# A transformer block on one core: the feed-forward's y turned by DMA, its tail spread over three engines, and two stage borders rewoven

## The chip, the cores and the metric

The program runs on one core of one Trainium2 chip. The metric is device microseconds for one execution. Before the change three runs gave 1199.7, 1199.9 and 1201.7 us, median 1199.9.

The engines are called PE (TensorE, matrix products and transposes), DVE (VectorE), ACT (ScalarE), POOL (GpSimd) and SP (SyncE, which here only issues transfers). Each works through its own list of instructions in order and waits on semaphores that the others raise.

## The reference, cut to what matters

64 images of 224 x 224 x 3 go through a patch embedding, one attention layer with fake quantisation and one feed-forward layer with activations rounded to 8 bits and ternary weights. There are 197 tokens of 192 values per image.

```python
h = _L0_tok_ref(x, W, b)                      # 196 patches an image -> 192 values
h = concatenate([cls_tok, h])                 # 197 tokens
h = h + _L0_attn_ref(_layernorm(h), ...)      # 12 heads of 64, every tensor fake-quantised
h = h + _L0_ffn_ref(_layernorm(h), ...)

def rmsnorm(x, g):          return x * rsqrt(mean(x*x) + 1e-6) * g
def activation_quant(x):    scale = 127 / max(max|x|, 1e-5);  return clip(round(x*scale), -128, 127) / scale
def weight_quant(w):        scale = 1 / max(mean|w|, 1e-5);   return clip(round(w*scale), -1, 1) / scale
def bitlinear(x, w, g):     return activation_quant(rmsnorm(x, g)) @ weight_quant(w).T
def _L0_ffn_ref(x, w_in, g_in, w_out, g_out):
    up, gate = split(bitlinear(x, w_in, g_in))     # 192 -> 2 * 512
    return bitlinear(silu(gate) * up, w_out, g_out)   # 512 -> 192
```

## The kernel before, in words

The three layers are three stages, each handed over through memory.

**Embedding, to about 215 us.** Fifteen packs of token tiles (SEQ; the last two are JOIN and LAST). For each tile PE sums six float32 products, DVE adds the bias and takes statistics, and DVE and POOL turn it into the quantised x. Each pack stores x (`x_int`) and h plus a bias (`h_res`), one transfer a tile. ACT issues the stores of the packs up to JOIN - 1, SP those of JOIN and LAST (`store_pack` of SP, lines 457 to 463: six transfers of x, then six of h).

**Join, about 215 to 255 us.** The first images of the attention stage are woven in beside the last packs. The attention's buffers lie over the embedding's (`big`), so after image step 1 DVE waits until every store of h and x has landed (lines 1113 to 1115) before it goes on with step 2.

**Attention, to about 860 us.** A software pipeline over images, `image_step(b)`: projections of image b + 1 or b + 2, scores and exponentials of b, softmax sums, normalising of b - 2 (line 1061), weighted values of b - 3, output projection of b - 4 and b - 5, and POOL adds the result into `h_res` in memory with an accumulating transfer (line 762). SP loads the turned x with a transposing transfer (`load_xT`, line 466), stores the inverse sums and loads them spread over all partitions (lines 485 and 492).

**Passage, about 860 to 920 us.** The last image steps (B to B + 4, with B = 64) only drain. The first steps of the feed-forward are placed between them by hand, engine by engine (the calls `images(...)` and `pairs(...)` at the end of each engine's block). SP loads the first `tin` only after all its image steps (lines 529 to 531).

**Feed-forward, to the end.** 50 pairs of 128-token tiles (the last holds 64 tokens). `pair_step(t)` is a software pipeline again: in one step, pair t gets its statistics and is centred, t - 1 its factors and zi, t - 2 is turned on PE and copied out, t - 3 goes through the 192 to 1024 product, silu, y, its square and y times g_out (yg), t - 4 gets the factors of y and yi (y rounded to int16), t - 5 is turned on PE (line 1297), copied out, multiplied by the output weights and given its residual (line 1043), t - 6 is stored. A step's work on DVE ends the factors with four tiny instructions (lines 968 to 979); ft (line 979) holds the factors that take the results of the products back to real size.

One ACT instruction (line 645) copies the turned x and the turned y together out of PSUM. Eight products that nobody reads (line 1322) follow each step on PE.

## Time and profile before

| | |
|---|---|
| median of three runs | 1199.9 us |
| the profiled execution, its own time | 1200.62 us |
| its span, first to last instruction | 1198.6 us |
| busy: PE, DVE, ACT, POOL | 1107.8, 1055.8, 923.2, 452.7 us |
| mean granted clock of TensorE | 0.977 |
| read from and written to HBM | 143.11 and 36.12 MB |

The shares over the whole span say little, because the stages differ: ACT does nothing in the first 190 us, and PE is busy almost throughout since fill-in products are among its work. Read the stages apart. A start in the timeline is in us from the first instruction. Engines overlap the end of one instruction with the start of the next by some 0.1 us, so what an instruction costs its engine is the distance between two starts and not quite its duration.

### The profile page before, as it was taken

The numbers are of one execution on the slowest core, as the hardware profiler recorded it, in microseconds if no ns is written. First come the engines' busy times: TensorE is split into PE (matmuls) and PEld (weight loads), VectorE is DVE, ScalarE is ACT, GpSimd is POOL, SyncE is SP. The second block draws the span as 40 slices with busy tenths as digits, with TensorE's granted clock in tenths as the row PEclk, the third lists the DMA queues.
The fourth block names the chain that finished last, engine by engine and source line by source line (L and its number), as shares of the span: only waits on it lengthen the run. The fifth ranks groups of instructions, "written<-read, shape, count | busy, mean of one in ns | idle before, by whom it ended". The sixth has DMA issues, their size and how long they took to land.

```text
span 1198.6 us, 31970 instructions
## 1 busy us (share of the span) xinstructions
PE 1107.8 (92%) x11182; PEld 674.8 (56%) x11182; DVE 1055.8 (88%) x2028; ACT 923.2 (77%) x1831; POOL 452.7 (38%) x486
## 2 busy tenths in 40 slices
PE   7999999879999999999999999999857888888888
PEld 6999998435555555555555555555433444444444
DVE  7687566479999999999999999999988999999996
ACT  0000002869999999999999999999738999999997
POOL 5644343102221123322111122121237777776774
PEclk9999999979999999999999999999958999999999
DMA  8998998336555566566655555555542333333332
GB/s 291 315 311 252 315 304 230 113 117 149 151 150 150 150 149 149 147 151 150 153 149 148 146 153 149 147 154 144 141 99 65 101 101 106 102 103 100 98 94 71
DMA packets 158436, 187.87 MB, mean 157 GB/s; under 512 B 42864, under 2 KB 119808, under 8 KB 158080
## 3 DMA queue, kind: packets, MB, share of 16 engines
q1 hardware_dynamic: 117408, 158.10, 42.4%
q0 software_dynamic: 15360, 9.70, 8.7%
q10 hardware_dynamic: 25536, 18.31, 4.7%
q8 instruction: 83, 1.36, 0.5%
q14 instruction: 49, 0.40, 0.1%
HBM read 143.11 MB, written 36.12 MB: 150 GB/s over the span
## 4 chain that ended last, share of the span: by engine, by line
PE 73%; ACT 10%; issue 8%; DVE 3%; DMA 2%; SPq 2%; POOL 2%; ACTq 0%; DVEq 0%; POOLq 0%
PE psum L1128 14%; PE psum L1186 12%; PE psum L1249 12%; PE psum L1219 7%; PE psum L1189 7%; PE psum L1202 6%; PE psum L1236 6%; PE psum L1307 5%; ACT yi L673 3%; ACT zi L681 2%; ACT big L666 2%; PE psum L1297 1%; DMA big<-xt 1%; PE psum L1287 1%; POOL big L790 1%
## 5 line engine op out<-in xcount | busy, mean ns | idle before, releaser
L1061 DVE TENSOR_TENSOR pi<-big 128x2364 int16<-128x2364 f32 (+1 forms) x128 | 333.5, 2605 | 10.1 <-DMA big<-z_row 9.8
L762 POOL DMA_DIRECT2D h_res<-att x128 | 142.0, 1214 | 526.4 <-ACT att L600 517.3
L624 ACT ACTIVATE big<-psum 128x788 f32<-128x788 f32 (+1 forms) x384 | 330.4, 862 | 3.0 <-PE psum L1236 2.6
L586 ACT ACTIVATE qki<-psum 128x394 int16<-128x394 f32 x384 | 172.5, 509 | 26.6 <-PE psum L1189 14.8
L1128 PE MATMUL psum<-big 128*128 128x192 f32 (+1 forms) x1128 | 185.1, 327 | 2.2 <-DMA big<-xt 2.0
L1128 PEld LDWEIGHTS psum<-big 128*128 128x128 f32 (+1 forms) x1128 | 180.3, 188 | 5.5 <-DMA big<-xt 2.6
L1249 PE MATMUL psum<-big,sa_hot 128*32 128x197 f32 (+1 forms) x3072 | 170.1, 339 | 7.9 <-DVE zt L1085 7.9
L586 ACT ACT_TABLE_LOAD x1 | 1.3, 1283 | 189.8 <-PE psum L1189 189.8
L790 POOL TENSOR_TENSOR big<-big,goutb 128x512 f32<-128x512 f32 (+1 forms) x99 | 123.7, 1270 | 55.5 <-DVE big L1033 55.5
L1236 PE MATMUL psum<-qkb 64*128 64x197 bf16 (+1 forms) x1536 | 129.7, 247 | 0.0
L595 ACT ACTIVATE vi<-psum 128x384 int16<-128x384 f32 (+1 forms) x256 | 115.7, 529 | 12.9 <-PE psum L1189 12.7
L1219 PE MATMUL psum<-big,vb 128*64 128x197 bf16 (+1 forms) x1536 | 105.7, 261 | 17.4 <-issue 15.5
L605 ACT ACTIVATE oi<-psum 128x394 int16<-128x394 f32 x192 | 102.8, 535 | 22.4 <-PE psum L1219 22.4
L851 DVE TENSOR_SCALAR big<-pi,lo,hi 128x2364 bf16<-128x2364 int16 (+1 forms) x128 | 115.0, 898 | 2.5
L1186 PE MATMUL psum<-xT,w1b 128*128 128x394 bf16 x384 | 105.8, 335 | 5.5 <-ACT qki L586 2.1
L1249 PEld LDWEIGHTS psum<-big,sa_hot 128*32 128x32 f32 (+1 forms) x3072 | 81.4, 110 | 50.9 <-issue 8.8
L1307 PE MATMUL psum<-winb,big 96*128 96x512 bf16 (+1 forms) x396 | 98.8, 394 | 0.0
L1219 PEld LDWEIGHTS psum<-big,vb 128*64 128x64 bf16 (+1 forms) x1536 | 63.0, 112 | 58.5 <-issue 55.6
L1322 PE MATMUL psum<-winb,big 96*128 96x512 bf16 x400 | 94.6, 379 | 0.0
L1236 PEld LDWEIGHTS psum<-qkb 64*128 64x128 bf16 (+1 forms) x1536 | 76.7, 104 | 30.8 <-issue 12.0
L860 DVE TENSOR_TENSOR big<-psum,tokb 128x192 f32<-128x192 f32 x98 | 34.4, 351 | 56.4 <-PE psum L1128 55.9
L1186 PE MATMUL psum<-w1b,xT 128*128 128x384 bf16 (+1 forms) x256 | 73.2, 338 | 8.2 <-ACT vi L595 1.4
(107 smaller groups left out, 1800.6 us busy)
## 6 DMA issues: line engine op xcount, KB each, us to landing
big<-z_row SPq DMA_DIRECT2D x192, 394.0 KB, 5.1
big<-xt SPq DMA_DIRECT2D x98, 384.0 KB, 4.5
tin<-h_res SPq DMA_DIRECT2D x49, 192.0 KB, 2.9
tres<-h_res SPq DMA_DIRECT2D x49, 192.0 KB, 2.5
out<-oo SPq DMA_DIRECT2D x49, 192.0 KB, 2.6
h_res<-big ACTq DMA_DIRECT2D x84, 96.0 KB, 4.4
h_res<-att POOLq DMA_DIRECT2D x64, 96.0 KB, 3.3
x_int<-big ACTq DMA_DIRECT2D x84, 64.0 KB, 4.2
```

Source lines behind the costliest of these rows:

```text
L586: act.activation(qki[:, k, :, :], psum[:, bank, 0:2 * N] .rearrange("p (c n) -> p c n", c=2), ACT.Copy, scale=factor[(F_Q, F_K)[b % 2]])\
L595: act.activation(vi[0:r, ip, t, half * W:(half + 1) * W], psum[0:r, bank, 0:W], ACT.Copy, scale=factor[F_V]).then_inc(evac[kind], 1)
L624: act.activation(ex[0:r, tri, t, 4 * g:4 * g + 4, :].rearrange("p (a h) n -> p a h n", a=2), psum[0:r, 2 * t:2 * t + 2, 0:2 * N] .rearrang ...
L762: pool.dma_start(h_res[bass.ds(b - 4, 1), t0:t0 + r, :].rearrange("a n d -> (a n) d"), att[0:r, par, t, :], accum_op=ALU.add).then_inc(s_a ...
L790: g.tensor_tensor(yg[0:r, oth, a, :], yy[0:r, a, 0:HID], goutb[0:r, :], ALU.mult)\
L1061: v.tensor_tensor(pi[0:r, t, :, 0:N], ex[0:r, it, t, :, :], zb[0:r, ip, :, :], ALU.mult).then_inc(s_pi, 1)
L1128: last = mm(psum[p0:p0 + r, bank_of_tile(i, s), 0:D], xring[:, s, c * 128 + p0:c * 128 + p0 + r], weight_of(cls, c), start=(c == 0), stop= ...
L1186: mm(psum[rows, bank, 0:n], left[:, 0], right[:, 0], start=True, stop=False)
L1219: last = mm(psum[i * DH:(i + 1) * DH, bank, c * N:(c + 1) * N], vb[0:r, (tri + d) % 3, t, head * DH:(head + 1) * DH], pT[0:r, im % 2, t, j ...
L1236: last = mm(psum[0:r, 2 * (w % 2) + i % 2, (i // 2) * N:(i // 2 + 1) * N], qk[po:po + DH, 6 + c, t0:t0 + r], qk[po:po + DH, c, 0:N], start ...
L1249: last = mm(psum[32 * j:32 * j + 32, 4, 0:N], sa_hot[0:r, w // 2, :], ex[0:r, it, t, 4 * (w // 2) + j, :], start=(w == 0), stop=(w == 5))
L1307: last = mm(psum[0:r, 2 * a + half, :], zT3[:, oth, a, c, 0:r], winb[:, c, half * HID:(half + 1) * HID], start=(c == 0), stop=(c == 1))
```

## The change

Five things are changed together.

1. y is turned by a transposing transfer of SP (from yi3 in SBUF to yTi, int16, laid over `qki`) in place of eight PE transposes. DVE converts it to bfloat16 (yT3, a single buffer) two steps later. ACT's copy takes the turned x alone. The pipeline is a step deeper (LAGS 8).
2. The output of a pair goes to two PSUM banks. DVE scales and adds tile 0 as before. ACT scales tile 1 into `osc` at the end of its step, and POOL adds the residual to it a step later.
3. POOL makes `ft` in place of DVE.
4. At the join, POOL issues the h stores of JOIN and LAST. DVE's wait for all stores moves from ahead of image step 2 to just ahead of the first write of the probabilities in it.
5. At the passage, the feed-forward's steps 0 to 5 are placed elsewhere among the last image steps, the first `tin` is loaded after image step B - 1, ACT loads the silu table ahead of its pair steps, and PE gets fill-in products in image steps B + 1 and B + 2 and in pair steps 0 to 2.

```diff
@@ SP
-                sp.wait_ge(s_hp, i + 1)
-                for s in range(PACK):
-                    sp.dma_start(tile_rows(h_res, i, s), hp[:, i % 2, s, :]).then_inc(s_h1[i % 2], 16)
...
+                if pair(5) or pair(7):
+                    wait_apart(sp, s_t["o_ready"], ...t - 6)
+                    wait_apart(sp, s_t["o_added"], ...t - 6)
+                if at := pair(5):
+                    sp.dma_start(tres[0:r, oth, 0:n, :], pair_rows(h_att, t - 5, r, n)).then_inc(s_t3b[oth], 16)
+                if at := pair(7):
+                    sp.dma_start(pair_rows(out, t - 7, r, n), oo[0:r, oth, 0:n, :]).then_inc(s_t3o[oth], 16)
+                if at := pair(4):
+                    wait_apart(sp, s_t["yi"], t - 3)
+                    wait_apart(sp, s_t["yT_read"], t - 5)
+                    sp.dma_start_transpose(yTi[:, par, 0:4 * n, 0:r], yi3[0:r, par, 0:n, :].rearrange("p a h -> p (a h)"))\
+                      .then_inc(s_ym[par], 16)
-            images(image_step, 0, B + 4)
+            images(image_step, 0, B - 1)
             wait_added(sp, 0)
             sp.dma_start(tin[:, 0, :, :], pair_rows(h_att, 0, 128, 2)).then_inc(s_t3[0], 16)
+            images(image_step, B, B + 4)
@@ ACT
-                    act.activation(zyT[:, par, :], turned.bitcast(i16)[:, 512:2048], ACT.Copy)\
+                    act.activation(zT3[:, par, 0:n, :, 0:r], psum[0:KH, 4, :].bitcast(i16)[:, 0:512]..., ACT.Copy)\
                        .then_inc(s_t["xT_read"], 1)
+                if (at := pair(6)) and at[1] == 2:
+                    act.wait_ge(s_t["o_summed"], t - 5)
+                    act.activation(osc[:, par, :], psum[:, 5, 0:D], ACT.Copy, scale=ft[:, (q + 2) % 4, 1, 1:2])\
+                       .then_inc(s_t["o_scaled"], 1)
+            act.activation(table[0:1, :], fac[0:1, 0:1], ACT.Silu)
@@ POOL
+                if i >= JOIN:
+                    pool.wait_ge(s_hp, i + 1)
+                    for s in range(PACK):
+                        pool.dma_start(tile_rows(h_res, i, s), hp[:, i % 2, s, :]).then_inc(s_hlast, 16)
+                if (at := pair(7)) and at[1] == 2:
+                    g.tensor_tensor(oo[:, oth, 1, :], osc[:, oth, :], tres[:, oth, 1, :], ALU.add)\
+                        .then_inc(s_t["o_added"], 1)
+                if pair(1) or pair(4):
+                    wait_apart(pool, s_t["step"], 3 * t - 1)
+                    g.tensor_tensor(ft[:, q, :, :], pt[:, oth, A127, :, :], wdeq4[:, :, :], ALU.mult)\
+                        .then_inc(s_t["dequant"], 1)
@@ DVE
-                        v.tensor_tensor(ft[:, q, :, :], V(A127), wdeq4[:, :, :], ALU.mult).then_inc(s_t["dequant"], 1)
+                if at := pair(6):
+                    dve.wait_ge(s_ym[par], loads_of(t - 6, par))
+                    wait(dve, s_t["o_summed"], t - 6)
+                    v.tensor_copy(yT3[:, 0:n, :, 0:r].rearrange("p a c n -> p (a c) n"), yTi[:, par, 0:4 * n, 0:r])\
+                     .then_inc(s_t["yT_read"], 1)
-                    for a in range(n):
-                        ins = v.scalar_tensor_tensor(oo[0:r, oth, a, :], psum[0:r, 6, a * D:(a + 1) * D], ...)
+                    v.scalar_tensor_tensor(oo[0:r, par, 0, :], psum[0:r, 6, 0:D], ft[0:r, (q + 2) % 4, 1, 0:1],
+                                           tres[0:r, par, 0, :], ALU.mult, ALU.add).then_inc(s_t["o_ready"], 1)
+                    if image == 0 and t == 0:
+                        dve.wait_ge(s_hlast, 32 * PACK)
+                        for p in range(2):
+                            dve.wait_ge(s_h1[p], stores_at(JOIN - 1 - (JOIN - 1 - p) % 2))
+                            dve.wait_ge(s_x1[p], stores_at(LAST - (LAST - p) % 2))
@@ PE
+                    if b in (B + 1, B + 2):
+                        pe.wait_ge(s_exp, U1 * B)
+                        keep_busy(3, 12)
-                        for c in range(4):
-                            last = nc.tensor.transpose(dst[:, a, c, 0:r], yi3[...], ident[0:r, 0:r])
-                    last.then_inc(s_t["yT_summed"], 1)
```

SP's list at the join, before (`xT` is the turned x of an image, `z_row` the inverse softmax sums, `x_int` and `h_res` the stores of a pack):

```order
L460 DMA x_int<-big 32x4x256 x6
L463 DMA h_res<-big 32x4x192 x6
L466 DMA_TRANSPOSE xT<-x_int 128x2x208
L485 DMA z_row<-zinv 4x197 x3
L492 DMA big<-z_row 128x788 x3
L460 DMA x_int<-big 32x4x256 x6
L463 DMA h_res<-big 32x4x192 x6
L466 DMA_TRANSPOSE xT<-x_int 128x2x208
```

And the same place now:

```order
L463 DMA x_int<-big 32x4x256 x6
L466 DMA_TRANSPOSE xT<-x_int 128x2x208
L486 DMA z_row<-zinv 4x197 x3
L493 DMA big<-z_row 128x788 x3
L463 DMA x_int<-big 32x4x256 x6
L466 DMA_TRANSPOSE xT<-x_int 128x2x208
```

Twelve issues have left SP's list; they stand in POOL's, six behind each of its last two packs.

DVE's list over one steady step of the feed-forward, before, from the residual of one step to the last factor of the next:

```order
L1043 SCALAR_TENSOR_TENSOR oo<-psum,ft,tres 128x192 x2
L998 BN_STATS st<-tin 128x6 x2
L1003 TENSOR_REDUCE pt<-zc 128x2
L1009 BN_AGGR mv<-st 128x2 x2
L1015 TENSOR_REDUCE pt<-big 128x1 x2
L968 TENSOR_TENSOR pt<-pt 128x4
L988 SCALAR_TENSOR_TENSOR zc<-tin,mv,ginb 128x192
L971 TENSOR_SCALAR pt<-pt 128x4
L988 SCALAR_TENSOR_TENSOR zc<-tin,mv,ginb 128x192
L974 RECIPROCAL pt<-pt 128x4
L979 TENSOR_TENSOR ft<-pt,wdeq 128x4
L977 TENSOR_TENSOR pt<-pt 128x4
```

And the same stretch now:

```order
L1069 SCALAR_TENSOR_TENSOR oo<-psum,ft,tres 128x192
L1020 CAST big<-qki 128x1024
L1026 BN_STATS st<-tin 128x6 x2
L1031 TENSOR_REDUCE pt<-zc 128x2
L1037 BN_AGGR mv<-st 128x2 x2
L1043 TENSOR_REDUCE pt<-big 128x1 x2
L991 TENSOR_TENSOR pt<-pt 128x4
L1010 SCALAR_TENSOR_TENSOR zc<-tin,mv,ginb 128x192
L995 TENSOR_SCALAR pt<-pt 128x4
L1010 SCALAR_TENSOR_TENSOR zc<-tin,mv,ginb 128x192
L998 RECIPROCAL pt<-pt 128x4
L1001 TENSOR_TENSOR pt<-pt 128x4
```

The conversion stands right behind the residual of the step before and ahead of the statistics, one of two residual instructions is gone, and so is line 979.

POOL's list over one steady step now (it was the same without lines 799 and 803):

```order
L783 TENSOR_TENSOR pt<-pt,neg_half 128x2
L789 TENSOR_SCALAR pt<-mv 128x2
L792 TENSOR_TENSOR pt<-pt,neg_half 128x2
L799 TENSOR_TENSOR oo<-big,tres 128x192
L803 TENSOR_TENSOR ft<-pt,wdeq 128x4
L811 TENSOR_TENSOR big<-big,goutb 128x512 x2
```

The residual of tile 1 and the factors stand between the powers and the two products with g_out.

## Rows read from the trace of the kernel before

**Rows 1.** Windows: start:end, us, busy us (instructions) of each engine, PEclk, DMA share, GB/s.
```profile
245.80:254.00 8.20, 7.85 (x60) 2.91 (x60) 8.13 (x8) 4.02 (x8) 0.00 (x0) 0.50 0.36 133
...
1020.00:1050.00 30.00, 26.55 (x185) 14.08 (x184) 28.30 (x92) 29.54 (x57) 20.93 (x25) 1.00 0.35 100
```
**Rows 2.** Waits, 205 to 262 us: who, for whom, us in all, times, longest.
```profile
DVE vb L851 <- DMA h_res<-big: 13.0, 1, 13.0
ACT vi L595 <- PE psum L1189: 12.7, 4, 8.6
```
**Rows 3.** Timeline of SP's queue at the join: start, us, instruction.
```profile
233.10 1.30 SPq L492 DMA_DIRECT2D big<-z_row  x3
234.45 4.00 SPq L460 DMA_DIRECT2D x_int<-big  x6
238.49 4.69 SPq L463 DMA_DIRECT2D h_res<-big  x6
```
**Rows 4.** Page, part 6: engine, op, count, KB each, median us from issue to landing.
```profile
big<-z_row SPq DMA_DIRECT2D x192, 394.0 KB, 5.1
```
**Rows 5.** Timeline of POOL's accumulating stores, two at a time.
```profile
856.95 2.63 POOL L762 DMA_DIRECT2D h_res<-att  x2 [6.30 <-ACT att L600]
864.14 1.78 POOL L762 DMA_DIRECT2D h_res<-att  x2 [4.57 <-ACT att L600]
```
**Rows 6.** Timeline of DVE at the passage.
```profile
880.57 0.62 DVE L998 BATCH_NORM_STATS2 st<-tin 128x6 f32<-128x192 f32 x2 [3.51 <-DMA tin<-h_res]
...
899.45 0.75 DVE L1033 SCALAR_TENSOR_TENSOR big<-psum,ft,big 128x512 f32<-128x512 f32 x1
...
920.46 1.41 DVE L1033 SCALAR_TENSOR_TENSOR big<-psum,ft,big 128x512 f32<-128x512 f32 x2
```
**Rows 7.** Timeline of ACT over one steady step.
```profile
1041.20 1.43 ACT L645 ACTIVATE big<-psum 128x1536 bf16<-128x1536 int16 x1
...
1043.67 1.34 ACT L673 ACTIVATE yi<-big,pt 128x512 int16<-128x512 f32 x2
...
1047.02 1.43 ACT L645 ACTIVATE big<-psum 128x1536 bf16<-128x1536 int16 x1
```
**Rows 8.** Timeline of POOL and DVE in the same step.
```profile
1047.39 0.69 POOL L773 TENSOR_TENSOR pt<-pt,neg_half 128x2 f32<-128x2 f32 x1 [0.54 <-ACT ysq L693]
...
1049.33 0.16 DVE L977 TENSOR_TENSOR pt<-pt 128x4 f32<-128x4 f32 x1
```
**Rows 9.** Waits, 960 to 1136 us (30 steps).
```profile
POOL big L790 <- DVE big L1033: 32.3, 30, 1.3
...
DVE pt L968 <- POOL pt L773: 7.9, 30, 0.4
```
**Rows 10.** Groups by line: shapes, count, busy us, mean ns of one, idle before.
```profile
L1043 DVE SCALAR_TENSOR_TENSOR oo<-psum,ft,tres 128x192 f32<-128x192 f32 x60 | 22.0, 408 | 0.0
...
L728 POOL TENSOR_TENSOR big<-big 128x192 f32<-128x192 f32 (+1 forms) x24 | 14.3, 594 | 13.4 <-DMA big<-w_tok 11.6
```
**Rows 11.** Single lines: duration ns min/median/max, first and last start, forms.
```profile
L651 ACT ACTIVATE big<-psum x4: 255/593/593, 894.8 to 1181.4; 96x512 bf16<-96x512 int16 x3, 96x128 bf16<-96x128 int16 x1
L907 DVE TENSOR_SCALAR woutb<-big x1: 359/359/359, 182.1 to 182.1; 128x768 bf16<-128x768 int16 x1
L907 DVE TENSOR_SCALAR winb<-big x1: 690/690/690, 132.8 to 132.8; 96x2048 bf16<-96x2048 int16 x1
```
**Rows 12.** DVE beside POOL at the join (timeline).
```profile
220.62 2.62 POOL L748 TENSOR_TENSOR big<-big,bb2b 128x1152 f32<-128x1152 f32 x1
222.22 1.66 DVE L851 TENSOR_SCALAR qkb<-qki,lo,hi 128x2364 bf16<-128x2364 int16 x1 [1.47 <-ACT qki L586]
...
230.76 0.90 DVE L851 TENSOR_SCALAR qkb<-qki,lo,hi 128x2364 bf16<-128x2364 int16 x1 [2.03 <-ACT qki L586]
```
**Rows 13.** The transposing load of x (line 466, 64 times), issue to landing.
```profile
DMA to landing us min/median/max: 2.5/5.6/7.1
```
**Rows 14.** Timeline of ACT at the end.
```profile
1194.23 0.39 ACT L657 ACTIVATE big<-psum 128x256 bf16<-128x256 int16 x1 [1.79 <-PE psum L1297]
```

More of the change, by code:

```diff
@@ L367, in pair_of, with over_pairs @@
             return pair
-        def over_pairs(eng, step):
+        def over_pairs(eng, step, start=None):
             first = 14
-            for t in range(EARLY, first):
+            for t in range(start or EARLY, first):
                 step(t, t % 2, t % 4)
@@ L1310, in pair_step @@
                         last.then_inc(s_t["hid"], 1)
-                if at := pair(5):
+                if at := pair(6):
                     r, n = at
-                    y_turned(t)
-                    wait(pe, s_t["o_ready"], t - 5)
+                    pe.wait_ge(s_t["yT_read"], t - 5)
+                    wait(pe, s_t["o_ready"], t - 6)
+                    wait(pe, s_t["o_scaled"], t - 6)
                     for a in range(n):
                         for c in range(4):
-                            last = mm(psum[0:r, 6, a * D:(a + 1) * D], yT3[:, par, a, c, 0:r], woutb[:, c, :],
+                            last = mm(psum[0:r, 6 - a, 0:D], yT3[:, a, c, 0:r], woutb[:, c, :],
                                       start=(c == 0), stop=(c == 3))
                     last.then_inc(s_t["o_summed"], 1)
-                if (pair(5) or pair(3)) and (not isinstance(t, int) or t > EARLY):
-                    for _ in range(8):
-                        mm(psum[:, 7, :], zT3[:, oth, 0, 0, :], winb[:, 0, 0:HID], start=True, stop=True)
+                if not isinstance(t, int) or EARLY <= t <= NPAIR + 2:
+                    keep_busy(7, 8)
+                elif t < 3:
+                    keep_busy(3, 4)
             for i in (JOIN, LAST):
```

154 lines of the change are left out of this document (69 added, 85 removed).

## The prediction

> **What bounds the kernel now.** I read the windows first, then the waits of the places where they show a gap, then single steps in the timeline. Three places matter.
>
> At the join nothing but transfers holds the chip: DVE stands 13.0 us until the last store of h has landed, and ACT 8.6 us behind it [rows 2]. The stores of the last pack leave SP one by one, six of x in 4.00 us and then six of h in 4.69 us [rows 3]. PE stands too, and the granted clock in the 8.2 us behind that gap is 0.50 (1.2 of 2.4 GHz), with ACT busy for only 4.02 us of them [rows 1].
>
> At the passage DVE stands 3.51 us for the first `tin`, with the last image's normalising queued behind it. Then the feed-forward needs 21.0 us, from 899.45 to 920.46, for its first three steps [rows 6].
>
> In the steady feed-forward ACT is busy 29.54 of 30 us [rows 1]. A step is the distance between two copies of line 645, 1047.02 - 1041.20 = 5.82 us [rows 7]. But there are two more limits just as close, and they decide what relief of ACT is worth:
> - A circle through three engines. yi starts when the factors are done. From yi to the end of the squares is 3.35 us (1043.67 to 1047.02) plus 0.1 for the last accumulator [rows 7]. The power on POOL starts at 1047.39, 0.28 us later, and from its start to the start of the last factor instruction are 1.94 us, with 0.16 for that one [rows 8]. Sum 3.45 + 0.28 + 1.94 + 0.16 = 5.83 us, which is the whole step.
> - DVE: it waits 7.9 / 30 = 0.26 us a step for that power [rows 9], so its own list takes 5.82 - 0.26 = 5.56 us.
>
> POOL waits 32.3 / 30 = 1.08 us a step for y [rows 9].
>
> **The join.** Twelve issues leave SP. Of these the six of pack LAST stood ahead of the landing that DVE waited for, and the six of JOIN ahead of everything else. On POOL the six of LAST cost up to 6 x 1.3 = 7.9 us (half of 2.63 each) from the end of the h add at 223.2 [rows 5, 12], so they are issued by 231 and landed by 236. The last stores are then those of x. The spread load of the inverse sums, at 233.10, waited for its own chain (the inverse sums, stored and landed) and hardly moves. Six x stores behind it end at 238.4, as now, and land by 241 [rows 3]. DVE no longer stands ahead of step 2: it does the conversion of v and turns the softmax sums at about 234, which is what PE stood for. Its first normalising waits for the spread load, 233.1 + 1.3 + some 4 = 238.5 (5.1 us from issue [rows 4]), in place of 246.3. I expect ACT's 8.6 us back and half of the 4 us that it lost at the low clock, against 1 to 3 us that it will wait for the next spread load: 8.5 us, bounds 5 and 11.
>
> POOL's stores write descriptors beside DVE's conversions; two accumulating stores took 2.63 us once against 1.78 [rows 5]. The Trainium skill speaks against this edit: by "SBUF — State Buffer", section "SBUF: two separate sides", GpSimd can't write descriptors while DVE is in a two-port mode. By it the six would end some 4 us later, at 235, still ahead of the x stores, so the sum is the same.
>
> **The passage.** `tin` is loaded early, which takes out the 3.51 us [rows 6]. Pairs 0, 1 and 2 move ahead of the last normalisings or between them: 1.5 + 2.3 + 2.3 us of DVE work that stood behind them, so the last probabilities come only some 1.5 us later than now, while the first 192 to 1024 product is ready to run as soon as the last values are done. The table load of 1.3 us leaves the path. By this the first y ends 4 to 6.5 us earlier (the range is the clock of that product, 1.7 or 3.5 us). The three steps that took 21.0 us would take 17.5 at the steady pace; I count 1 us of these 3.5 as won. Together 6 us, bounds 2 and 9. The fill-in products cost nothing where PE has nothing to do; if they stood ahead of work that is ready they would cost 12 x 0.21 us.
>
> **ACT in the steady step.** The copy of 1536 columns, 1.43 us, becomes one of 512 columns, 0.59 [rows 7, 11]. The scaling of tile 1 is new: 192 columns, by the distance per column between these two rows 0.3 to 0.45; I take 0.38. ACT's list is then 5.82 - 0.84 + 0.38 = 5.36 us. That alone frees 0.46 us.
>
> **DVE in the steady step.** One residual instruction goes, 22.0 / 60 = 0.37 us [rows 10], and ft, 0.1. The conversion of 1024 columns is new. The nearest rows are 0.36 us for 768 columns and 0.69 for 2048 [rows 11]; I take 0.42. DVE's list is 5.56 - 0.47 + 0.42 = 5.51 us.
>
> It can also be held. Beside POOL's add of 1152 columns (220.62 to 223.24) a conversion of 2364 columns took 1.66 us, alone 0.90 [rows 12]: it did its work only when POOL was nearly through, some 0.2 us ahead of POOL's end. The new conversion comes 1.0 us after the first y, and just then POOL is 0.9 us into the first of two products with g_out, 1.27 us each. I count 0.1 to 0.4 us of hold, as much as the rest of the first product, so 5.6 to 5.9 us.
>
> The same rule is in the Trainium skill, "SBUF — State Buffer", section "Who interferes with whom": the pair of ports is locked for a whole instruction, and the one that comes second is blocked. Our row agrees but for the 0.2 us at the end. It also says this for a DVE instruction with two SBUF inputs beside a reading one of GpSimd, which would touch the centring and POOL's new add; by it the step would be longer by up to the add's 0.5 us where they meet.
>
> **POOL in the steady step.** The add of 192 columns costs 0.59 [rows 10], the factors 0.2, both inside the 1.08 us that it waits for y [rows 9]. Some 0.2 us is left, and with the three register writes of the waits perhaps none. When the first product with g_out starts later, the conversion is held longer.
>
> **The circle.** Of its terms only ft leaves, 0.1: 5.73 us. So the step can't fall below about 5.7 whatever ACT gains. With DVE at 5.6 to 5.9, and POOL full, I take a step of 5.83 us, no change: 43 steps x 0 = 0, bounds 43 x -0.12 = -5 and 43 x +0.3 = +13.
>
> **The transfers.** A transposing load of x lands 5.6 us after issue, 2.5 at least [rows 13]. The new one has 2.5 times the elements. It has from yi in one step to the conversion two steps on, over 8 us, and SP has three other issues of 0.4 us a step. Bound below 0; above, if it takes SP over 4 us to issue, `tin` comes late and the step grows by as much. I take 0.
>
> **The end.** One more step, and the last turn goes through a transfer: 5 us in place of 2.2 (1.79 for PE and 0.39 for the copy [rows 14]). +2.5 us, bounds 1 and 5.
>
> **Sum.** 1200.6 (the profiled execution) - 8.5 - 6 + 0 + 2.5 = 1188.6. That execution is 0.7 above the median, so 1188.
>
> **Rivals.**
> - A, the step falls to the circle's 5.7: the conversion meets no product, or is held for 0.1. Then 1188 - 5 = 1183. For it: the hold is short by the rows. If the circle too gives way since the engines shift against each other, and ACT's list decides at 5.4, it is 43 x -0.4 = -17: 1171. Against it: the three engines' sums are all within 0.3 us.
> - B, slower: the conversion is held through both products with g_out. These stand back to back, and if POOL takes the second before DVE gets in, the hold is 1.4 us and DVE's list 6.9 to 7.1. The step becomes 7.1: 43 x 1.3 = +56, 1244. For it: the rows show only a single POOL instruction, never two, and the conversion waits at this place in every step. Against it: DVE has asked first, and POOL seems to let go 0.2 us ahead of its end. From a hold of 0.28 us a step above my forecast (12 / 43) on the change loses.
> - C, in between: POOL's new add meets the centring and the last factor in each step, or SP's transfer makes `tin` late. +0.35 us a step, +15: 1203.
> - D, the join gives little, since the next spread load (its chain begins behind the x stores) stops DVE again: -3 in place of -8.5, 1194.
>
> **Chances.** Forecast with D 0.57, A 0.22 (of it 0.05 for 1171), C 0.11, B 0.10. 0.2% is 2.4 us, about what can be told from no change here. Faster 0.81, same 0.05, slower 0.14. The range from 1173 to 1206 leaves out B, the lowest part of A and a little of C.
>
> **What would show it.** Right: the gap of ACT at 240 us is under 3 us; the first y of pair 0 comes 13 to 16 us earlier; steps of line 1060 are 5.7 to 5.95 us apart; the conversion's mean is 0.5 to 0.8 us, above the 0.42 that it needs, and POOL's wait for y is near 0. Wrong: a mean of the conversion over 1.5 us (B); DVE waiting for `tin` or for the turned y (the transfers); ACT with no idle time at a step of 5.4 (A's lower part); any gap over 5 us at the join.

## The result, and the profile after

| | before | after |
|---|---|---|
| median on the same chip | 1200.8 us | 1215.7 us |
| the profiled execution, its own time | 1200.62 us | 1215.72 us |
| its span | 1198.6 us | 1213.9 us |
| mean granted clock | 0.977 | 0.962 |

The ratio of the times is 1.0127, with an interval from 1.0108 to 1.0145. The forecast was 1188 us, 12 us faster than before, with a range from 1173 to 1206. The change is 15 us slower: wrong in sign.

The two spans differ by 15.3 us. Three instructions of DVE exist in both traces and split this sum: the last normalising of the attention (885.66 before, 880.73 after), and the first and the last y (899.45 and 1188.01 before, 890.65 and 1198.26 after).

| part | before to after | forecast |
|---|---|---|
| join: the last normalising starts earlier | -4.9 | -8.5 (5 to 11) |
| passage: the first y against it, 13.8 to 9.9 us | -3.9 | -6 (2 to 9), 1 of it in the first three steps behind |
| 49 steps of the feed-forward, 288.6 to 307.6 us | +19.0 | 0 (-5 to +13) |
| from the last y to the end, 10.6 to 15.6 us | +5.0 | +2.5 (1 to 5) |

**The join.** DVE's timeline and SP's queue after the change (start, us, instruction, idle time before it):

```profile
239.34 2.62 DVE L1090 TENSOR_TENSOR pi<-big 128x2364 int16<-128x2364 f32 x1 [1.28 <-DMA big<-z_row]
...
248.31 0.41 DVE L1120 STREAM_TRANSPOSE zinv<-zti 128x224 f32<-128x224 f32 x1
252.51 2.62 DVE L1090 TENSOR_TENSOR pi<-big 128x2364 int16<-128x2364 f32 x1 [3.79 <-DMA big<-z_row]
```
```profile
233.72 3.86 SPq L463 DMA_DIRECT2D x_int<-big  x6
241.89 1.24 SPq L466 DMA_TRANSPOSE xT<-x_int  x1
243.22 1.67 SPq L486 DMA_DIRECT2D z_row<-zinv  x3
245.98 1.29 SPq L493 DMA_DIRECT2D big<-z_row  x3
```

The 13.0 us of DVE [rows 2] are gone and the first normalising starts 7.0 us earlier. The second starts only 4.2 us earlier. DVE had its inverse sums ready at 238.06 (the trace has L1120 at 237.65 for 0.41), but SP issued nothing until 241.89, since its wait for all stores stands there, then issued the load of xT, and only then stored the sums.

**The steady step.** The windows, in the form of [rows 1]:

```profile
1000.00:1060.00 60.00, 48.94 (x263) 25.00 (x262) 58.00 (x162) 50.83 (x115) 48.34 (x67) 0.89 0.55 135
```

ACT has 9 us of idle time in 60, as the change meant it to have. DVE is busy 58.0 of 60. The granted clock is 0.89, where it was 1.00 before [rows 1]; e8 below asks whether that matters. One step on DVE, from y to y:

```profile
1038.29 1.41 DVE L1060 SCALAR_TENSOR_TENSOR big<-psum,ft,big 128x512 f32<-128x512 f32 x2
1039.62 0.41 DVE L1069 SCALAR_TENSOR_TENSOR oo<-psum,ft,tres 128x192 f32<-128x192 f32 x1
1039.94 0.81 DVE L1020 CAST big<-qki 128x1024 bf16<-128x1024 int16 x1
1040.67 0.61 DVE L1026 BATCH_NORM_STATS2 st<-tin 128x6 f32<-128x192 f32 x2
...
1041.81 1.24 DVE L1043 TENSOR_REDUCE pt<-big 128x1 f32<-128x512 f32 x2
1043.18 0.16 DVE L991 TENSOR_TENSOR pt<-pt 128x4 f32<-128x4 f32 x1
...
1043.69 0.41 DVE L1010 SCALAR_TENSOR_TENSOR zc<-tin,mv,ginb 128x192 f32<-128x192 f32 x1
1044.02 0.17 DVE L998 RECIPROCAL pt<-pt 128x4 f32<-128x4 f32 x1
1044.23 0.35 DVE L1001 TENSOR_TENSOR pt<-pt 128x4 f32<-128x4 f32 x1
1044.50 0.75 DVE L1060 SCALAR_TENSOR_TENSOR big<-psum,ft,big 128x512 f32<-128x512 f32 x1
```

That is 6.21 us without a wait. POOL and ACT in the same step:

```profile
1039.20 2.67 POOL L811 TENSOR_TENSOR big<-big,goutb 128x512 f32<-128x512 f32 x2 [0.71 <-DVE big L1060]
1042.21 0.70 POOL L783 TENSOR_TENSOR pt<-pt,neg_half 128x2 f32<-128x2 f32 x1 [0.33 <-ACT ysq L691]
...
1043.27 0.69 POOL L792 TENSOR_TENSOR pt<-pt,neg_half 128x2 f32<-128x2 f32 x1
1043.93 0.62 POOL L799 TENSOR_TENSOR oo<-big,tres 128x192 f32<-128x192 f32 x1
```
```profile
1038.48 1.33 ACT L671 ACTIVATE yi<-big,pt 128x512 int16<-128x512 f32 x2 [0.86 <-DVE pt L1001]
...
1044.61 0.72 ACT L671 ACTIVATE yi<-big,pt 128x512 int16<-128x512 f32 x1 [0.73 <-DVE pt L1001]
```

Two meetings can be read here. The conversion (1039.94) comes while POOL is in its first product (1039.20 to 1040.5) and lasts 0.73 us to the next start. And the last factor instruction, four columns wide, comes while POOL's add runs (1043.93 to 1044.55) and ends with it at 1044.58. yi waits for just that instruction. Two instructions of this kind can also run side by side: the centring (L1010, two inputs in SBUF) started at 1043.69, 0.42 us into POOL's power (1043.27, 0.69 us), and took its usual 0.41. The groups of 28 steps (960 to 1136 us):

```profile
L1020 DVE CAST big<-qki 128x1024 bf16<-128x1024 int16 x28 | 20.9, 748 | 0.0
...
L799 POOL TENSOR_TENSOR oo<-big,tres 128x192 f32<-128x192 f32 x28 | 16.9, 604 | 0.0
...
L1001 DVE TENSOR_TENSOR pt<-pt 128x4 f32<-128x4 f32 x28 | 11.3, 403 | 1.0
```

403 ns for L1001, where the same instruction (L977) took 0.16 before [rows 8]. In all 30 steps from 950 to 1140 us it ended 0.01 to 0.03 us behind POOL's add.

**The end** shows the hold of the conversion most plainly, since there it once meets a product and once nothing. DVE, then POOL:

```profile
1199.25 1.37 DVE L1020 CAST big<-qki 128x1024 bf16<-128x1024 int16 x1
...
1202.81 0.42 DVE L1020 CAST big<-qki 128x1024 bf16<-128x1024 int16 x1
...
1209.12 0.41 DVE L1069 SCALAR_TENSOR_TENSOR oo<-psum,ft,tres 64x192 f32<-64x192 f32 x1 [3.60 <-DMA out<-oo]
```
```profile
1199.08 1.26 POOL L811 TENSOR_TENSOR big<-big,goutb 64x512 f32<-64x512 f32 x1 [0.96 <-DVE big L1060]
1200.35 0.69 POOL L783 TENSOR_TENSOR pt<-pt,neg_half 64x1 f32<-64x1 f32 x1
```

The same conversion takes 0.42 us alone and 1.37 when it starts 0.17 us behind POOL's product. It ended at 1200.62, 0.28 us behind the product. If its 0.42 us of work stand at its end, it began them 0.14 us ahead of the product's end. The last residual also waits 3.60 us for an earlier store.

**The passage.** In three steps from the first y (890.65, 897.00, 903.37, 912.65) the last has 9.3 us. POOL:

```profile
906.82 3.65 POOL L772 DMA_DIRECT2D h_res<-att  x4
909.15 2.08 POOL L783 TENSOR_TENSOR pt<-pt,neg_half 128x2 f32<-128x2 f32 x1
```

Four accumulating stores stand in a row ahead of a power, and DVE waited 3.38 us for it (its L991 started at 911.42).

### The profile page after: what moved, and what is told of

Its sections match the earlier page's. It is cut to its first block, busy times and chain, and to the rows that moved or that the text cites. A ratio compares the mean times of both kernels' runs of the same rounds, so it can differ in the third digit from the quotient of the medians.

```text
span 1213.9 us, 31866 instructions
## 1 busy us (share of the span) xinstructions
PE 1105.7 (91%) x10814; PEld 668.1 (55%) x10814; DVE 1081.0 (89%) x1976; ACT 900.2 (74%) x1877; POOL 502.0 (41%) x600
## 4 chain that ended last, share of the span: by engine, by line
PE 67%; DVE 14%; issue 8%; DMA 4%; ACT 3%; POOL 3%; SPq 1%; DVEq 1%; ACTq 0%; POOLq 0%
PE psum L1154 14%; PE psum L1212 12%; PE psum L1275 12%; PE psum L1245 7%; PE psum L1215 7%; PE psum L1228 6%; PE psum L1262 6%; DVE pt L1043 3%; DVE big L1060 2%; DVE big L1020 2%; PE psum L1324 2%; POOL big L811 1%; DVE zc L1010 1%; DVE st L1026 1%; DMA big<-xt 1%
## 5 line engine op out<-in xcount | busy, mean ns | idle before, releaser
L772 POOL DMA_DIRECT2D h_res<-att x128 | 138.8, 1196 | 501.8 <-ACT att L609 492.6
L811 POOL TENSOR_TENSOR big<-big,goutb 128x512 f32<-128x512 f32 (+1 forms) x99 | 132.3, 1357 | 35.2 <-DVE big L1060 35.2
L1324 PE MATMUL psum<-winb,zT 96*128 96x512 bf16 (+1 forms) x396 | 112.4, 435 | 0.4 <-DVE big L1060 0.4
L1303 PE MATMUL psum<-winb 96*128 96x512 bf16 x428 | 109.3, 401 | 0.0
L671 ACT ACTIVATE yi<-big,pt 128x512 int16<-128x512 f32 (+1 forms) x99 | 66.0, 713 | 33.5 <-DVE pt L1001 33.4
```

The source lines that it names most:

```text
L772: pool.dma_start(h_res[bass.ds(b - 4, 1), t0:t0 + r, :].rearrange("a n d -> (a n) d"), att[0:r, par, t, :], accum_op=ALU.add).then_inc(s_a ...
L811: g.tensor_tensor(yg[0:r, oth, a, :], yy[0:r, a, 0:HID], goutb[0:r, :], ALU.mult)\
L1324: last = mm(psum[0:r, 2 * a + half, :], zT3[:, oth, a, c, 0:r], winb[:, c, half * HID:(half + 1) * HID], start=(c == 0), stop=(c == 1))
```

## The experiments

A "step" below is the distance between the starts of y on DVE, the mean over 30 of them (11th to 41st). The conversion and the last factor are means of the group from 960 to 1136 us. These three are of the profiled execution alone, which was the fastest of four in e4 and e6 and the slowest of four in e2. The ratio is to the kernel before on the same chip; the experiments ran on four chips, so compare their ratios rather than their medians. e3, e4 and e5 leave out a part of the work.

| kernel | step, us | conversion, us | last factor, us | median, us | ratio to before, interval |
|---|---|---|---|---|---|
| before | 5.86 | - | 0.16 | 1200.8 | |
| after | 6.26 | 0.75 | 0.40 | 1215.7 | 1.0127 (1.0108 to 1.0145) |
| e1 join alone | 5.87 | - | | 1196.5 | 0.9955 (0.9941 to 0.9969) |
| e2 join and passage | 5.87 | - | 0.16 | 1192.7 | 0.9917 (0.9901 to 0.9934) |
| e3 small conversion | 6.24 | 0.52 | 0.44 | 1216.4 | 1.0121 (1.0087 to 1.0155) |
| e4 small add | 6.17 | 0.75 | 0.17 | 1212.0 | 1.0092 (1.0076 to 1.0109) |
| e5 both small | 5.98 | 0.52 | 0.18 | 1202.7 | 1.0008 (0.9992 to 1.0024) |
| e6 add behind | 6.18 | 0.76 | 0.16 | 1215.5 | 1.0119 (1.0102 to 1.0136) |
| e7 both moved | 6.29 | 0.85 | 0.16 | 1217.8 | 1.0141 (1.0124 to 1.0158) |
| e8 more fill-in | 6.26 | 0.75 | 0.44 | 1217.8 | 1.0132 (1.0111 to 1.0154) |
| e9 sums first | 5.87 | - | | 1194.2 | 0.9946 (0.9931 to 0.9961) |
| e10 stores apart | 5.87 | - | | 1198.2 | 0.9977 (0.9963 to 0.9992) |
| e11 conversion ahead of y | 6.25 | 0.43 | 0.18 | 1226.2 | 1.0216 (1.02 to 1.0232) |
| e12 ft on POOL | 5.92 | - | 0.18 | 1197.8 | 0.9974 (0.9963 to 0.9985) |
| e13 and fill-in first | 6.15 | 0.43 | 0.18 | 1221.5 | 1.0171 (1.0142 to 1.0199) |
| e14 and transfer first | 6.05 | 0.43 | 0.19 | 1204.4 | 1.0026 (1.0009 to 1.0043) |

**e1 and e2: what the two stage borders are worth.** Edit: the kernel before, with item 4 of the change (e1), and with items 4 and 5 (e2). The pair step stays as it was.

```diff
@@ e1, DVE (and POOL's and SP's lines of item 4)
-            images(image_step, 1, 1)
-            for p in range(2):
-                dve.wait_ge(s_h1[p], stores_at(LAST - (LAST - p) % 2))
...
-            images(image_step, 2, B + 2)
+            images(image_step, 1, B + 2)
@@ e2, POOL (and the other engines' orders of item 5)
-            images(image_step, -2, B + 1)
-            pairs(pair_step, 0, 1)
...
+            pairs(pair_step, 3, 5)
+            images(image_step, B + 2, B + 3)
+            over_pairs(pool, pair_step, 6)
```

> The kernel before with the join's part alone (h stores of the last two packs from POOL, DVE's wait moved). In the changed kernel the first normalising of the attention starts 7.0 us earlier (239.34 against 246.34), but the second only 4.2 us (252.51 against 256.76), and the last one 5.0 us (880.7 against 885.7). Theory: the join is worth 5.0 us, not the 8.5 of the prediction, since DVE waits 3.8 us for the next spread load: 1195.8 against 1200.8. Rival (the forecast's size is right and the later loss comes from elsewhere in the attention stage, such as the early tin or the fill-in products): 1192. Rival (POOL's stores hold DVE and nothing is left): 1199 or more.

> The kernel before with the join's and the passage's parts, but with y turned on PE, one ACT copy and the whole tail on DVE as before: the feed-forward's steady step is not touched. In the changed kernel the first y starts 8.9 us earlier than before (890.65 against 899.45, less a little for its first step). Theory: all the loss is in the steady step and the end, so this kernel beats both: 1200.8 - 8.9 = 1192, with a steady step of 5.83. Rival: the passage's gain hangs on the deeper pipeline or is given back in the first steps: 1196 (the join alone).

Measured 1196.5 and 1192.7, where the kernel before took 1201.7 on the same chip: the first reading of each. In e1 the second normalising starts at 252.34, as in the changed kernel. So the two borders gain 9 us (10 by the ratio), and the feed-forward part of the change loses 23 to 25 (1215.7 - 1192.7, or 1.0127 / 0.9917). e2 beats both kernels.

**e3, e4, e5: the conversion, the add, both.**

```diff
-                    v.tensor_copy(yT3[:, 0:n, :, 0:r]..., yTi[:, par, 0:4 * n, 0:r])
+                    v.tensor_copy(yT3[:, 0, 0, 0:r], yTi[:, par, 0, 0:r])
```
```diff
-                    g.tensor_tensor(oo[:, oth, 1, :], osc[:, oth, :], tres[:, oth, 1, :], ALU.add)
+                    g.tensor_tensor(oo[:, oth, 1, 0:24], osc[:, oth, 0:24], tres[:, oth, 1, 0:24], ALU.add)
```

> The changed kernel with the conversion cut to 128 of its 1024 columns (7/8 of the turned y stay unconverted, so the outputs of the feed-forward are not the reference's); its place, its waits and the transfer stay. Theory (DVE's list sets the step, the conversion with its hold costs it 0.73 us): the conversion falls to 0.1 to 0.2 us and the step from 6.2 to 5.7 to 5.8, where the circle through ACT and POOL takes over; 48 steps x -0.4 = -19: about 1197. Rival 1 (the transposing transfer or the lower granted clock sets the step): no change, 1215. Rival 2 (the conversion is only its 0.42 of work, no hold): the step falls by 0.3, 1201; here its hold shows in that it stays over 0.3 us although it is small.

> The changed kernel with POOL's residual add cut to 24 of its 192 columns from the third pair on (the other columns of the second output tile are then not the reference's); its place and its waits stay. Theory (the add holds DVE's last factor instruction, 0.40 us against 0.16 before, and delays its start by 0.1): line 1001 falls to 0.16 and the step by 0.2 to 0.3; 48 x -0.25 = -12: 1204. Rival (the add is not in DVE's way and what it frees on POOL is only idle time): line 1001 stays at 0.4, 1215. Rival 2 (POOL is the bound, by its own length): the step falls by 0.4, 1197.

e3 was a miss: 1216.4, no change, where 1197 was expected. The conversion of 128 columns was expected at 0.1 to 0.2 us and takes 0.52: most of that is the wait beside POOL's product. It is still 0.23 us less than before, and what this takes off DVE's list comes back as a wait for the power. In e3, 960 to 1136 us:

```profile
DVE pt L991 <- POOL pt L783: 9.5, 28, 0.7
```

and two steps of its factor (DVE) and add (POOL):

```profile
1037.45 0.61 DVE L1001 TENSOR_TENSOR pt<-pt 128x4 f32<-128x4 f32 x1
...
1043.90 0.34 DVE L1001 TENSOR_TENSOR pt<-pt 128x4 f32<-128x4 f32 x1
```
```profile
1037.45 0.59 POOL L799 TENSOR_TENSOR oo<-big,tres 128x192 f32<-128x192 f32 x1
...
1043.63 0.59 POOL L799 TENSOR_TENSOR oo<-big,tres 128x192 f32<-128x192 f32 x1
```

The factor starts 0.00 and 0.27 us behind the add and ends 0.02 behind it each time: whenever it comes, it is held until the add is over. That is on the circle, and with DVE's list relieved it keeps the steps at 6.1 to 6.3.

e4 brought 3.7 us where 12 were expected. The factor is free (0.17), and DVE's wait for the power is gone:

```profile
DVE pt L992 <- POOL pt L783: 0.5, 2, 0.3
```

There DVE's list is 1040.16 to 1046.29 = 6.13 us from y to y without a wait. So either limit alone holds the step near 6.2.

> The changed kernel with the conversion cut to 128 of 1024 columns and POOL's residual add cut to 24 of 192 (outputs of the feed-forward not the reference's). With the conversion cut alone the step stayed at 6.09 to 6.3 us: the last factor instruction still took 0.35 to 0.61 beside the add, and yi started 0.04 after it. With the add cut alone the factor took 0.16 but the first factor instruction came 0.25 us later, behind DVE's list. Theory (two separate limits of the same length, the circle with the held factor and DVE's list with the held conversion): with both cut the step falls to 5.75 to 5.9, and the time by 48 x 0.3 to 0.4 = 14 to 19 us: 1200, of it some late first inputs of silu left. Rival (a third limit, PE at the lower granted clock, holds it): step over 6.05, 1210 or more.

e5 bears this out: 5.98 and 1202.7, 13.0 less than the changed kernel (14 by the ratios). Of the two cuts alone, one brought nothing and the other 3.7 us. What e5 still lacks to e2, 10 us, is half in the steps (49 x 0.11 = 5.4) and half behind the last y (15.0 us against 10.6). What holds its step above 5.87 no run isolates; its conversion is still held (0.52).

**e6, e7: whole kernels with the meetings moved.** Edit of e6 on POOL, and of e7 also on DVE (the conversion behind L1037):

```diff
+                    g.tensor_tensor(ft[:, q, :, :], pt[:, oth, A127, :, :], wdeq4[:, :, :], ALU.mult)
                 if (at := pair(7)) and at[1] == 2:
...
+                        wait_apart(pool, s_t["factors"], t)
                     g.tensor_tensor(oo[:, oth, 1, :], osc[:, oth, :], tres[:, oth, 1, :], ALU.add)
```

> The changed kernel, whole, with POOL's add moved behind DVE's last factor instruction (POOL makes ft first, then waits for the factors, then adds). The add then starts 0.4 us later than now and ends 0.2 us or less ahead of the products with g_out. Theory: line of the factors falls from 0.40 to 0.16, but DVE's list with the held conversion stays the second limit, so the step falls by only 0.05 to 0.1, as in the run with the small add: 1211. Rival (the circle is the only limit): 48 x -0.25, 1204. Rival 2 (the add now holds y on DVE or delays the products): 1216 or more.

> The changed kernel, whole, with both moves: POOL's add behind the factors, and DVE's conversion behind line 1037 instead of ahead of the statistics, 1.8 us later, when POOL's two products with g_out are done or nearly so. Theory (held conversion and held factor are the two limits): conversion from 0.75 to 0.45, factor from 0.40 to 0.16, step 5.85 to 5.9: 48 x -0.28 = -13: 1203. Rival 1 (the conversion meets the end of the second product and is held as before): 1210. Rival 2 (the turned y now comes late for the product with the output weights, and ACT's scaling of tile 1 late with it): 1216 or more.

e6 has the step of e4, as expected, but its median is 1215.5 (expected 1211), within the noise of no change. The step is that of its fastest execution, 1212.6. e7 missed its 1203: the factor fell to 0.16, but the conversion rose to 0.85, the mechanism of its first rival, with a time (1217.8) nearer that of its second. Its DVE and POOL rows:

```profile
1042.00 0.91 DVE L1039 CAST big<-qki 128x1024 bf16<-128x1024 int16 x1
```
```profile
1039.32 0.59 POOL L805 TENSOR_TENSOR oo<-big,tres 128x192 f32<-128x192 f32 x1 [0.44 <-DVE pt L1003]
1040.13 2.50 POOL L813 TENSOR_TENSOR big<-big,goutb 128x512 f32<-128x512 f32 x2 [0.22 <-DVE big L1062]
```

The add, now behind the factors, and the products follow each other until 1042.63, and the conversion meets the second product in place of the first.

**e8: the granted clock.**

```diff
-                    keep_busy(7, 8)
+                    keep_busy(7, 12)
```

> The changed kernel with 12 fill-in products a step instead of 8 (nothing else). In the changed kernel the granted clock of the feed-forward is 0.83 to 0.93 where it was 1.00 before, and in a quarter of the steps one silu starts late behind PE and the step has 6.3 to 6.9 us. PE has 1.6 us a step of idle time for four more products of 0.22 each. Theory (the low clock costs 1 to 2 of the 19 us of the steady part by such steps): clock near 1.00, long steps gone, 48 x -0.08 = -4: 1211. Rival (the clock is only a sign of waiting): 1215. Rival 2 (the products stand ahead of the real ones): 1220.

Its windows:

```profile
1000.00:1060.00 60.00, 52.40 (x314) 27.20 (x315) 58.33 (x167) 50.96 (x116) 48.91 (x68) 1.00 0.58 139
```

The clock is 1.00 (2.4 GHz) and the step is as long as at 0.89, and the time is not shorter (1.0132 against 1.0127, within the noise): the first rival. So the low clock was a sign of PE's waiting and not a cause of the loss.

**e9, e10: more from the borders.** On e2: SP stores the sums of image step 2 ahead of its waits (e9); also POOL's stores of image B + 3 stand two pair steps later (e10).

```diff
+                if b == 2:
+                    for g in range(3):
+                        sp.dma_start(z_row[g, :, :], zinv[g:128:32, 0:N]).then_inc(s_zrow, 16)
                 if b == 2:
                     sp.wait_ge(s_hlast, 32 * PACK)
@@ e10, POOL
             pairs(pair_step, 3, 5)
-            images(image_step, B + 2, B + 3)
-            over_pairs(pool, pair_step, 6)
+            images(image_step, B + 2, B + 2)
+            pairs(pair_step, 6, 7)
+            images(image_step, B + 3, B + 3)
+            over_pairs(pool, pair_step, 8)
```

> The kernel with join and passage alone (the second experiment), and SP stores the inverse sums of image step 2 ahead of its wait for all stores of the join. In the changed kernel this store left at 243.22, though DVE had made the sums by 238.06, because SP stood at the wait until 241.89 and then issued the load of xT; DVE then waited 3.79 us for the spread load behind it. Theory: this wait is what ate 3.5 of the 8.5 us forecast for the join; with the store early the spread load can leave right behind the wait and land some 3 us earlier: 1192.7 - 2.5 to 3.5 = 1189.5. Rival (the load of xT or the next spread load becomes late instead, and the loss is moved): 1192.5.

> As the one before (inverse sums first), and POOL's accumulating stores of the last two images are taken apart: those of B + 3 stand two pair steps behind those of B + 2. In the changed kernel and in the one with join and passage alone, four such issues in a row take 3.65 us at the passage, the power behind them takes 2.1, and DVE waits 3.4 to 3.5 us for it; that step lasts 9.3 us. Theory: two issues (1.8 us) lie mostly in POOL's wait of 1.0 us for y, so each of the two steps loses about 1 us in place of 3.4 in one: 1.5 us won, 1188. Rival (each pair of issues costs a step its full 1.8 us and the longer power again): 1189.5, no change.

e9's step did what it should: the second normalising starts at 247.89 instead of 252.16, after a wait of 0.83 in place of 3.7 us, and the last of the attention at 875.77 instead of 881.36. Yet its median is 1194.2, no better than e2's (another chip; the intervals of the ratios overlap). Its six times go from 1188.7 (the profiled one) to 1197.3, the fastest with the highest mean clock (0.993) and the slowest with the lowest (0.984), so the gain may be lost at the passage; no run settles it.

e10 did what it should, too: DVE's longest wait for the power fell from 3.1 us (e9) to 1.4. But its median is 1198.2, and its trace shows a new wait. POOL, SP and DVE:

```profile
920.65 1.86 POOL L774 DMA_DIRECT2D h_res<-att  x2
```
```profile
924.17 0.37 SPq L532 DMA_DIRECT2D tin<-h_res  x1
```
```profile
926.66 0.62 DVE L1014 BATCH_NORM_STATS2 st<-tin 128x6 f32<-128x192 f32 x2 [7.23 <-DMA tin<-h_res]
```

SP loads `tin` of a pair only when the images that it covers have been added into `h_res`. With the last stores two steps later, one such load leaves at 907.89 and the next only at 924.17 (in e9 they leave 6 to 9 us apart there). DVE stands 7.23 us for it, and that one step lasts 12.96 us. That is more than the 1.7 us won at the power. The granted clock from 890 to 900 us also differs (0.50, in e9 0.83); no run shows whether the order of POOL has a part in that.

**e12: ft alone.** On e2:

```diff
@@ DVE
-                        v.tensor_tensor(ft[:, q, :, :], V(A127), wdeq4[:, :, :], ALU.mult).then_inc(s_t["dequant"], 1)
@@ POOL
+                    wait_apart(pool, s_t["step"], 3 * t - 1)
+                    g.tensor_tensor(ft[:, q, :, :], pt[:, oth, A127, :, :], wdeq4[:, :, :], ALU.mult)
```

> The kernel with join and passage alone (the second experiment), and POOL makes ft in place of DVE, as in the change: this shortens DVE's list and the circle by 0.11 us a step, POOL has 1.1 us of idle time a step. ACT is busy 59.0 of 60 us there. Theory (three limits within 0.1 us: the circle, ACT's list at 5.8): ACT's list holds the step, at most 0.05 is won: 1192.7 - 48 x 0 to 0.05 = 1191.5. Rival (the circle alone sets the step): 48 x -0.11 = -5: 1187.5. Rival 2 (POOL's instruction holds the last factor instruction on DVE as the add does, though it has only four columns): +0.1 a step, 1197.

1197.8 and a step of 5.92, 0.05 longer: no gain. The 5 us between the medians are twice what the step gives, while the two profiled executions are alike (1195.5 and 1196.0), so a part of the loss stays open. The last factor takes 0.18 in place of 0.16, so its second rival is there, but small. DVE's rows (e12):

```profile
1042.49 0.16 DVE L988 RECIPROCAL pt<-pt 128x4 f32<-128x4 f32 x1
1042.68 0.16 DVE L991 TENSOR_TENSOR pt<-pt 128x4 f32<-128x4 f32 x1
```

From the reciprocal to the last factor are 0.19 us without ft and 0.20 with it between them (1043.11 to 1043.31 in the kernel before). ft lay in the time between the reciprocal and the factor that needs its result, and cost nothing there.

**e11, e13, e14: a whole kernel without the meetings.** In e11 the conversion stands between the last factor and y, for pair t - 5, and POOL's add waits for it. e13 puts PE's fill-in ahead of the output product, e14 also the transposing transfer ahead of SP's other two.

```diff
@@ DVE, behind factors(3)
+                if at := pair(5):
+                    dve.wait_ge(s_ym[oth], loads_of(t - 5, oth))
+                    v.tensor_copy(yT3[...], yTi[:, oth, 0:4 * n, 0:r]).then_inc(s_t["yT_read"], 1)
@@ POOL, behind ft
+                        wait_apart(pool, s_t["yT_read"], t - 4)
+                    g.tensor_tensor(oo[:, par, 1, :], osc[:, par, :], tres[:, par, 1, :], ALU.add)
```

> The changed kernel, whole, with DVE's conversion between the last factor and y, for the pair before (so the pipeline is as deep as before the change), and POOL's add behind that conversion. POOL runs nothing there, as its add waits for the conversion and its products for y. Theory (what cost the steady step is the meeting of DVE's conversion and factor with POOL's two-input instructions, and not their work): conversion 0.42, factor 0.16, DVE's list 5.7, the circle 5.75 plus some 0.1 to 0.2 since y starts 0.4 later: step 5.9 to 6.0 in place of 6.27 on the mean, 48 x -0.3 = -14, and one step less in the pipeline, -4: 1198. Rival 1 (the conversion waits for the transfer, which now has one step less): over 1216. Rival 2 (the circle runs through y, its products and y_amax, all 0.42 later): step 6.2, 1211.

e11 was a miss: 1226.2, where 1198 was expected. The conversion took 0.43 and the factor 0.18 as hoped, but two new waits came (960 to 1136 us):

```profile
PE psum L1337 <- DVE big L1052: 40.3, 24, 2.1
...
DVE big L1052 <- DMA qki<-yi: 6.2, 19, 0.7
```

The step is as long as in the changed kernel. Behind the last y it takes 20.7 us in place of 15.6, with waits of 3.3 and 2.4 us for the transfer.

The edits of e13 and e14:

```diff
@@ e13, PE
+                    keep_busy(7, 8)
                 if at := pair(5):
                     pe.wait_ge(s_t["yT_read"], t - 4)
...
-                    keep_busy(7, 8)
@@ e14, SP
+                    sp.dma_start_transpose(yTi[...], yi3[...]).then_inc(s_ym[par], 16)
                 if pair(4) or pair(6):
                     wait_apart(sp, s_t["o_ready"], ...)
...
-                    sp.dma_start_transpose(yTi[...], yi3[...]).then_inc(s_ym[par], 16)
```

> As the eleventh experiment (conversion between the last factor and y, add behind it), and PE runs its eight fill-in products ahead of the product with the output weights instead of behind it. There the conversion took 0.43 us and the factor 0.21, as hoped, but the step stayed at 6.25: PE stood 1.3 to 1.7 us for the conversion, with the fill-in, the turning of x and the next product queued behind, so that silu came 0.3 to 0.4 us late, and DVE waited 0.2 us a step for the transfer. Theory (without the two meetings the step is set by the queue of PE alone): with the fill-in ahead PE reaches the next pair 1.5 us earlier, step 6.0 to 6.05: 1226 - 48 x 0.22 = 1215. Rival (the transfer, one step less ahead, holds it): step over 6.15, 1222.

> As the thirteenth, and SP issues the transposing transfer ahead of the residual's load and the store, whose wait for POOL's add delays it there; it then leaves some 0.8 to 1.2 us earlier and lands ahead of the conversion. Theory: DVE's wait for the transfer goes, step 5.9 to 6.0: 1226 - 48 x 0.3 = 1212 or below. Rival (the circle with y 0.4 us later sets the step by now): as the thirteenth, within 0.03 us a step.

e13 fell to its rival: the step went to 6.15, but the median only to 1221.5 (expected 1215), and DVE waited 9.7 us for the transfer. e14: that wait is gone, step 6.05 and 1204.4, 11.3 less than the changed kernel with the same work (12 by the ratios). DVE, then POOL:

```profile
1039.11 0.16 DVE L1003 TENSOR_TENSOR pt<-pt 128x4 f32<-128x4 f32 x1
1039.29 0.43 DVE L1052 CAST big<-qki 128x1024 bf16<-128x1024 int16 x1
1039.63 1.40 DVE L1062 SCALAR_TENSOR_TENSOR big<-psum,ft,big 128x512 f32<-128x512 f32 x2
```
```profile
1039.89 0.60 POOL L805 TENSOR_TENSOR oo<-big,tres 128x192 f32<-128x192 f32 x1 [0.84 <-DVE big L1052]
1040.45 2.49 POOL L813 TENSOR_TENSOR big<-big,goutb 128x512 f32<-128x512 f32 x2
```

Neither is held. y and POOL's products come later for it, and DVE waits for the power again (9.8 us in 28 steps). It is still 12 us slower than e2, 6 of them from the first y to the last (296.5 against 290.7) and 6 behind (17.0 against 10.6).

## Why the prediction was wrong

**The step that failed** is the forecast of the steady step: "with DVE at 5.6 to 5.9, and POOL full, I take a step of 5.83 us, no change". It was 6.26, above even the upper bound (5.83 + 0.3 = 6.13). POOL was not full either: it still waited 17.8 us in 28 steps for y, 0.64 a step. Two sums behind that sentence failed together, DVE's list and the circle. Of its terms:

- *ACT in the steady step*: right. It got its idle time. That this was worth nothing fits the two other limits, which stood just as close; no run relieves ACT alone.
- *DVE, the conversion*: right in both parts. 0.42 us of work, as taken, and 0.33 of hold (mean 0.75), inside the 0.1 to 0.4 counted.
- *DVE, "ft, 0.1"*: wrong. Its removal freed nothing (e12), neither on the list nor on the circle.
- *DVE's own list, "5.82 - 0.26"*: too short. In the kernel before, the first factor instruction's wait for the maximum of y (the reduction in front of it) was hidden in the wait for the power. Without that wait the two starts are 1.37 us apart (L1043 at 1041.81, L991 at 1043.18), for 1.24 of busy time: 0.13. So the list is 5.60 (6.02 less 0.42 in the step from 1043.52) - 0.33 (residual) + 0.73 + 0.13 + some 0.06 in front of y: 6.19. The step shown has 6.21, e4 6.13. So this limit alone reaches the upper bound. Of the 0.35 by which 6.19 exceeds the prediction's 5.51 + 0.33, ft has 0.10 and this wait 0.13.
- *The circle, "5.73"*: the failure of mechanism. It was 5.86 (3.72 from yi to the power, 0.90 to the first factor, 1.04 to the last, 0.20 to yi). The last factor grew by 0.24, so it became 6.10, and e3, with DVE's list relieved, has steps of 6.1 to 6.3. The prediction counted the add at 0.59, "inside the 1.08 us that it waits for y", and asked no further whom it stops while it runs.

The prediction named this in rival C, "POOL's new add meets the centring and the last factor in each step", with +0.35 us a step, 1203 and a chance of 0.11 (shared with a late `tin`). The factor was met, and the step grew by 0.40; the centring was not held (0.42 us on the mean, as before). The time is above that 1203 because join, passage and end together brought 3.8 us where 12 were forecast, and because there are 49 steps where 43 were counted. Its rule was in the sentence on the Trainium skill, "SBUF — State Buffer", section "Who interferes with whom": a DVE instruction with two SBUF inputs beside a reading one of GpSimd. The trace agrees for the add, by 0.40 against 0.16 us; beside POOL's power it does not show in the centring (0.41 us, started 0.42 us into it). Rival C got a small chance since the meeting was looked for in lengths of lists and not in starts. In the kernel before, POOL's instruction in front of the place of the new add is this:

```profile
1048.44 0.92 POOL L782 TENSOR_TENSOR pt<-pt,neg_half 128x2 f32<-128x2 f32 x1
```

It ends at 1049.36, and the last factor starts at 1049.33 [rows 8]. An add put right behind it had to meet that factor.

Rival B did not come: a conversion gets in between two products and holds up the second (the pair took 2.67 against 2.50 us).

**The join**: 4.9 where 8.5 was forecast: rival D in part. Its place was right (the next spread load) and the wait was 3.8 us. The cause was SP's own wait at image step 2, past which the store of the sums had to go; e9 took the wait away.

**The passage**: inside the bounds. In the prediction's own terms the first y came 3.9 us earlier against the join, where about 5 were counted, and the three steps behind it took 22.0 us instead of 21.0, where 20 were counted. The second part is the four stores in a row on POOL, which the new order put together (DVE waited 3.38 us there). The first y came 8.8 us earlier in all, not the 13 to 16 that the prediction gave as a sign.

**The end**: +5.0, at the upper bound. The trace has DVE's 1.37 us for a held conversion and 3.60 us for a store there; no run takes them apart.

**The transfers**, taken as 0: right in the steady steps of the changed kernel, where DVE waits for none of them. They land 2.3 to 4.9 us after issue.

## What to carry to other kernels

Work moved to an idle engine is not free because it fits into the idle time: ask which instruction of the other engine it meets, and whether that one is on the circle. When two limits lie within 0.1 us of each other, a cut of one shows little or no gain, and only the cut of both tells (e3, e4, e5). An instruction that stands between two dependent ones may cost nothing, so its removal gains nothing. A change of several parts is best priced and tried part by part: here the two borders were worth 9 us, and the feed-forward part cost 23. And when a wait is taken away, look for what the move delays: e10 cut a wait of 3.1 us to 1.4 and made one of 7.2.

## What the runs showed of the hardware

- A four-column tensor_tensor of DVE (L1001) was held by POOL's tensor_tensor of 192 columns until its end (0.34 to 0.61 us in place of 0.16; ends 0.01 to 0.03 us apart in every step from 950 to 1140 us of the changed kernel and of e3). Beside POOL's power of two columns (0.69 us) DVE's centring, with two inputs in SBUF as well, was not held (0.41 us). The conversion ended 0.28 us behind the end of POOL's product and takes 0.42 alone (end of the changed kernel).
- A held conversion of 128 columns took 0.52 us, one of 1024 columns 0.75, of which 0.42 is its time alone.
- The transposing transfer of 128 x 1024 elements occupied SP's queue for 1.25 us an issue and landed after 2.3 to 4.9.
- Four accumulating stores of POOL in a row took 3.65 us, and the power behind them 2.08 (0.70 in a steady step).
